# Ten bf16 products of 128x512 into an unread PSUM bank, behind the second scaled product of the last stage

## The reference, cut to what matters

```python
def _L0_cond2_ref(x, A, B, adapter_ids):
    Bx = jnp.einsum('bni,bri->bnr', x, B[adapter_ids])
    return jnp.einsum('bnr,bor->bno', Bx, A[adapter_ids])
...
    h = _layernorm(vit_embeds, gamma, beta)
    h = _dyn_quant_linear(h, w1, b1)
    h = jax.nn.gelu(h, approximate=False)
    h = _dyn_quant_linear(h, w3, b3)
...
    x = x + _L0_attn_ref(_L0_cond_ref(x, ...), ...)
    x = x + _L0_ffn_ref(_L0_cond2_ref(x, ...), ...)
```

## Time and profile before

| | us |
|---|---|
| median of 3 runs | 602.52 |
| lowest, highest | 602.12, 605.37 |
| the profiled execution, its own time | 599.33 |
| span of its instructions | 597.5 |
| mean granted TensorE clock over the span | 0.99 |

### The profile page before, as it was taken

The page is one execution under the profiler, slowest core; times in us unless marked ns, Lnnn a source line. Parts: engine busy times, 40 slices in busy tenths (PEclk is TensorE's granted clock), DMA queues, the critical chain, the costliest instruction groups (busy, mean ns, idle before and its releaser), DMA issues. The chain is left out here.

```text
span 597.5 us, 10369 instructions
## 1 busy us (share of the span) xinstructions
PE 568.8 (95%) x3107; PEld 430.4 (72%) x3107; DVE 495.5 (83%) x643; ACT 327.4 (55%) x877; POOL 401.0 (67%) x410
## 2 busy tenths in 40 slices
PE   6999979999999999999999999999999999987985
PEld 4545658888887788888878887888878888773342
DVE  2974558998999799979997999799979998867696
ACT  2142456556554655565556555655565555557594
POOL 3004288698679867976897689769966997751053
PEclk9999999999999999999999999999999999999699
DMA  9931334512451245124412442254123422100003
GB/s 277 250 70 35 82 95 125 128 49 57 133 127 47 58 128 132 42 60 135 123 45 60 131 114 53 55 146 103 51 66 107 105 47 59 36 1 0 1 2 142
DMA packets 38173, 51.93 MB, mean 87 GB/s; under 512 B 12101, under 2 KB 20453, under 8 KB 38149
## 3 DMA queue, kind: packets, MB, share of 16 engines
q1 hardware_dynamic: 35076, 45.89, 29.6%
q10 hardware_dynamic: 2592, 4.53, 2.3%
q0 software_dynamic: 480, 1.22, 0.6%
HBM read 28.55 MB, written 2.10 MB: 51 GB/s over the span
## 5 line engine op out<-in xcount | busy, mean ns | idle before, releaser
L1015 DVE SCALAR_TENSOR_TENSOR accT<-pair,so_now,accT 128x1024 f32<-128x1024 f32 x125 | 157.6, 1278 | 20.6 <-PE pair L1284 19.8
L1001 DVE SCALAR_TENSOR_TENSOR raw_q<-pair,sc_now,raw_q 128x1024 f32<-128x1024 f32 x90 | 115.5, 1283 | 3.5
L1283 PE MATMUL pair<-ctx_hi,wo 128*128 128x512 f32 x256 | 104.9, 410 | 2.6 <-issue 1.5
L677 ACT ACTIVATE probs<-flow,negmax 128x128 f32<-128x128 f32 x248 | 87.3, 369 | 34.3 <-DVE negmax L966 34.3
L1283 PE MATMUL pair<-h_hi,wq 128*128 128x512 f32 x240 | 100.9, 420 | 1.8 <-ACT raw_q L720 1.7
L1284 PE MATMUL pair<-ctx_lo,wo 128*128 128x512 f32 x256 | 100.4, 392 | 0.0
L1284 PE MATMUL pair<-h_lo,wq 128*128 128x512 f32 x240 | 94.4, 393 | 0.0
L528 POOL TENSOR_TENSOR probs<-probs,rowinv 128x512 f32<-128x512 f32 x64 | 66.7, 1042 | 28.3 <-DVE rowinv L988 28.3
L509 POOL TENSOR_TENSOR qT<-rope_c,rope_s 128x512 f32<-128x512 f32 x62 | 79.4, 1280 | 4.4
L497 POOL TENSOR_TENSOR rope_s<-swap_q,consts 128x512 f32<-128x512 f32 x62 | 80.3, 1295 | 2.1 <-DMA swap_q<-raw_q 2.1
L497 POOL TENSOR_TENSOR rope_c<-raw_q,consts 128x512 f32<-128x512 f32 x62 | 78.5, 1286 | 0.6
(11 more groups left out here) (229 smaller groups left out, 989.3 us busy)
## 6 DMA issues: line engine op xcount, KB each, us to landing
swap_q<-raw_q SPq DMA_DIRECT2D x62, 256.0 KB, 3.5
wq_i<-in_L_attn_qw_q SPq DMA_DIRECT2D x8, 1024.0 KB, 6.0
wo_i<-in_L_attn_qw_o SPq DMA_DIRECT2D x32, 256.0 KB, 2.7
swap_k<-raw_k SPq DMA_DIRECT2D x14, 256.0 KB, 3.6
wkv_i<-in_L_attn_qw_k SPq DMA_DIRECT2D x8, 256.0 KB, 3.8
wkv_i<-in_L_attn_qw_v SPq DMA_DIRECT2D x8, 256.0 KB, 4.0
out<-probsT SPq DMA_DIRECT2D x8, 256.0 KB, 2.0
stage<-in_x ACTq DMA_DIRECT2D x4, 256.0 KB, 4.6
```

What stands on the lines that cost most here:

```text
L677: e = act.activation(probs[:, 0, f, seq(b)], bank[:, seq(b)], ACT.Exp, bias=negmax[:, f, b:b + 1], accum_out=rowsum[:, f, b:b + 1])
L1001: dve.scalar_tensor_tensor(out=into, in0=flat(pair[pair_of(h, (kind, j), last)][:, :, :]), scalar=sc_now[:, scale_slot(kind, h), j:j + 1], ...
L1015: dve.scalar_tensor_tensor(out=a, in0=flat(pair[pair_of(h, (O, c), last)][:, :, :]), scalar=so_now[:, (h if c == 0 else h - 1) % 2, c:c + ...
L1283: pe.matmul(into[:, f, :], w, upper[:, half[f]], start=True, stop=False)
```

## The change

TensorE gets ten more products between `scaled_product(1)` and `scaled_product(2)`. Each multiplies the bf16 identity (`ident_b`, 128x128) by 512 columns of the first layer's bf16 weights (`ffT`) into bank 3, with start and stop set, and no semaphore is counted. Nothing reads the bank before `turn_rows(1, 0)` writes it again. Ahead of the ten stands a wait for the second square, the last reader of what bank 3 held. Nothing else is changed.

```diff
             scaled_product(0)
             turn_residual(0)
             scaled_product(1)
+            pe.wait_ge(squares_done, 2)
+            for _ in range(10):
+                pe.matmul(banks[3], ident_b[:, :], ffT[:, 0, 0, :], start=True, stop=True)
             scaled_product(2)
             turn_residual(1)
             scaled_product(3)
```

## The result

| | before | changed |
|---|---|---|
| median, us | 602.32 (4 runs) | 594.66 (4 runs) |
| lowest, highest | 600.44, 605.37 | 593.75, 595.24 |
| profiled execution, span | 599.33, 597.5 | 594.74, 592.6 |
| mean granted clock over the span | 0.990 | 0.998 |

The ratio of the two is 0.9867, with a 95% interval of 0.9824 to 0.991: faster by 0.9 to 1.8%, and by more than the 0.5% that can be told from no change. The forecast was 597.8 us, the range 594.8 to 602.2. (Ratios leave out executions over 1.5% above the fastest of their kernel and are not the quotient of the two medians; medians and extremes here are of all.)

A forecast was written before the change was run, and what follows sets the result against it. TensorE at half clock behind a 2.09 us gap was taken to bound the last stage. Full clock gains 4.7 us after the ten's 0.05: profile 599.33 to 594.6, median 602.52 to 597.8 us, range 594.8 to 602.2.

The forecast's parts named there:

- The bound: Last stage, from 553.87 us: bound by TensorE only because its clock is halved; VectorE waits for it five times, 4.81 us.
- The cost of the ten: In the gap before the third scaled product: ten take 2.15 us, the gap is 2.10, so that product is 0.05 late.
- The gain of the clock: Behind the gap: with full clock held, VectorE reaches the third layer's `scale_product` sooner, a gain of 4.7 us.
- the carry to the median: Whole kernel: the timed median's 3.2 us above the profiled execution was kept for the changed kernel, giving 597.8 us.
- rival B: Timed executions of the kernel before need not lose what the profiled one does: 600 to 602.5 us; chance 0.13.
- Rival C: The half-clock stretch is longer in timed executions: gain up to 7.9 us, time 594.6 us; chance 0.07.
- The argument for holding: At the gap: clock stays full once filled, since similar work ahead kept it; gain taken near the 4.9 us upper bound.
- Rival A: Behind the gap: the clock only falls later, at about 558 us; 602.4 to 602.7 us, or 599.5 if it recovers; chance 0.15.
- rival D: In the gap: the ten run at half clock, take 4.3 us, third scaled product 2.2 late; 604.7 us; chance 0.03.
- The rule on transposes: Trainium skill: transposes don't engage full clock, which would give 602.4 to 602.7 or 599.5 us; the set-up's trace disagreed.

The follow-up runs named there:

- e13: The kernel before the change, unchanged, profiled once more: 601.27 us, clock 0.986.
- e9: The changed kernel with its ten products, run again for 12 executions: median 596.09 us, ratio 0.9914 to the kernel before.
- e18: The changed kernel with its ten products, run a third time: median 595.17 us, ratio 0.9911 to the kernel before.
- e3: Against the changed kernel, two f32 products of 32 rows in place of the ten: median 600.46 us, ratio 1.0017 to the kernel before.
- e7: Against the changed kernel, the ten bf16 products use only 32 rows: median 600.58 us, ratio 1.0002 to the kernel before.
- e10: Against the changed kernel, four more products in two idle times ahead of the low products, all into bank 7: median 596.86 us.
- e4: Against the changed kernel, sixteen f32 transposes in place of the ten: median 597.94 us, ratio 0.9949 to the kernel before.

## Why the prediction was right and wrong

- **The bound.** Right. The stage was bound by TensorE at half clock; with the clock held, VectorE's waits went from 4.81 us to 0.62.
- **The cost of the ten.** Small, as said: 0.16 us late instead of 0.05. The first norm ended at 554.39 us and the third scaled product began at 554.55. From the end of the second scaled product (552.36) to there it is 2.19 us for the ten, and without them the gap would have been 2.03.
- **The gain of the clock.** 4.64 us between the profiles for 4.7. Of the five waits the last was 0.62 us and not 0.15, but the distance on VectorE from the first norm on shrank as forecast.
- **The step that failed: the carry to the median, "the median of the timed runs is 3.2 us above the profiled execution for a reason that the profile doesn't show, and I carry it over".** The term was put at 3.2 us for the changed kernel too, without a reason. It measured -0.1 us there in the first four executions (594.66 against 594.74) and 0.5 in 28. In the kernel before, 1.8 of the 3.2 us are real (601.1 - 599.33), and they are mostly time at half clock: the profiled execution was of the shortest class (0.990, 143 of 144 executions are at or below that), and where a typical one loses more, the change gives more back (6.3 us in e13's profile). The other 1.4 us were the draw of three executions. The hint stood in the argument against rival B, that the profiled execution was the fastest; it speaks for C, and I used it only against B.
- **Rival C (0.07)** had this mechanism, and its 594.6 us is what was measured. That it met the number is partly luck, since it gave back all of the 3.2 us. Over all executions the gain is 601.1 - 595.3 = 5.8 us, between the forecast's 4.7 and C's 7.9, and chip by chip 4.6 (e9) and 5.6 (e18). The forecast's miss of 3.1 us is about 1.4 for a kernel before that was drawn high, 0.6 for four executions of the ten without a long fall, and 1.1 for what the change gives back beyond 4.7.
- **The argument for holding: "the 2.09 us of idle is the only thing in front of the fall that the stretch ahead of it lacked".** Wrong. e3 and e7 took the idle time away and changed nothing; what the ten add is 128 rows at work. Its conclusion, a clock held throughout, came true in 12 of 28 executions; with the short falls, most of the gain is there in 21.
- **Rival A (0.15) and rival D (0.03)** both exist, as single executions: e9's late fall, and, in the kernel with fourteen, e10's ten at half clock. I had treated them as alternatives for the whole kernel; they are shares of its executions. A range over executions' medians should have mixed them.
- **Rival B** is out: all 144 executions of the kernel before have a clock of 0.991 or less, where a profile without a fall has 0.998.
- **The rule on transposes** had been set aside on the evidence of the set-up. That evidence is weaker than I took it for. The granted clock of the profile reads 1.00 from 4 to 10 us, so the rise there is read from durations alone (1.06 to 0.60 us), at a time when transfers kept the DMA engines busy (a share of 0.94 and more). e4 is the test, and it shows a half-way truth.

## What to carry to other kernels

Before a difference between a profiled execution and a median is carried over to the changed kernel, ask whether the two may differ by the very thing that the change removes. A profiled execution that is faster than every timed one may be a sample from the short end, and then the gain in the median is larger than its own. If TensorE's clock falls in a stage of thin products (32 rows here), try to fill the stage's gaps with full-height products that nobody reads. Here the count that just fits the gap was best of five, eight, ten and twenty; thin filler did nothing, late filler nothing clear of noise, and twenty gave back more than half of what ten gain. Judge such a change by a dozen executions with their clocks, since four can all come out well.

## What the runs showed of the hardware that was not expected

- A gap of TensorE filled for 2.1 us with products of 32 rows left clock and time as an idle gap does (median clock of e3 0.9875, of e7 0.985, of the kernel before 0.986); ten products with 128 rows in e7's place gave 0.996.
- The time at half clock varies between executions of one and the same program: 10.2, 13.7 and 17 us in the profiles of the kernel before, mean clocks from 0.975 to 0.991.
- Two falls in one stage are possible within 7 us, at 552.2 and 559.0, with most of ten dense products between them (e10).
- Sixteen f32 transposes in the gap gave a median clock of 0.991, between nothing and ten products.
- Twenty dense products did not hold the clock better than ten (median 0.992 against 0.996). Whether they hold it worse is not settled.
